# One head's query of the second attention moved from the attention block into the preparation block before it

## The reference

```python
h = _layernorm(x, axis=-1) * (1 + ca) + sa
q_c = rmsnorm(h @ w_qa, g_qa)                       # 192 wide
q = (q_c @ w_qb).reshape(b, s, NH, ND + RD).transpose(0, 2, 1, 3)
q_nope, q_rope = q[..., :ND], q[..., ND:]
kv = h @ w_kva
k_c, k_rope = rmsnorm(kv[..., :KVR], g_kva), kv[..., KVR:]
...
q_rope = q_rope * cos + rotate_half(q_rope) * sin
...
attn = softmax(query @ key.T * QK ** -0.5)          # 512 x 512 for each of 2 x 32 heads
x = x + ga * (attn @ v) @ w_o
```

## Time and profile before

| what | us |
|---|---|
| three runs: median | 921.61 |
| three runs: lowest, highest | 920.1, 924.47 |
| profiled execution, its own time | 919.29 |
| profiled execution, span from first to last instruction | 917.1 |
| TensorE busy in the span | 825.5 (90%) |
| VectorE, GpSimd, ScalarE busy | 681.8, 538.3, 536.6 |
| mean granted TensorE clock | 0.953 of full |

### The profile page before, as it was taken

The page is one execution under the profiler, slowest core; times in us unless marked ns, Lnnn a source line. Parts: engine busy times, 40 slices in busy tenths (PEclk is TensorE's granted clock), DMA queues, the critical chain, the costliest instruction groups (busy, mean ns, idle before and its releaser), DMA issues.

```text
span 917.1 us, 15064 instructions
## 1 busy us (share of the span) xinstructions
PE 825.5 (90%) x4560; PEld 543.2 (59%) x4560; DVE 681.8 (74%) x1322; ACT 536.6 (59%) x1158; POOL 538.3 (59%) x481
## 2 busy tenths in 40 slices
PE   3899994599996985799999999999899999999997
PEld 1678873577774763456565656565565656565443
DVE  4758987644453462989898989899998989898662
ACT  5658873724223772666666666666566666666522
POOL 3324342012122213999888888888788888887313
PEclk8789997799998895999999999999999999999999
DMA  8440000745233440466666666666567766666511
GB/s 331 168 156 1 2 2 2 217 130 173 88 103 126 136 129 18 119 157 155 153 154 154 156 154 155 150 155 153 129 153 184 184 148 155 152 154 146 130 37 69
DMA packets 91460, 120.08 MB, mean 131 GB/s; under 512 B 30386, under 2 KB 41650, under 8 KB 91380
## 3 DMA queue, kind: packets, MB, share of 16 engines
q1 hardware_dynamic: 66804, 85.54, 33.8%
q10 hardware_dynamic: 24576, 33.59, 14.8%
HBM read 41.45 MB, written 2.10 MB: 47 GB/s over the span
## 4 chain that ended last, share of the span: by engine, by line
PE 45%; DVE 9%; issue 5%; ACT 1%; ACTq 1%; POOL 1%; DMA 0%; POOLq 0%; DVEq 0%; SPq 0%
PE bank L1477 11%; PE bank L1464 6%; PE bank L1465 5%; PE bank L1466 5%; PE bank L1491 4%; PE bank L1493 3%; PE bank L1492 3%; PE bank L1535 3%; DVE blk L1595 2%; DVE cT_lo L1669 2%; DVE stage_a L1571 2%; ACTq L1406 1%; DVE nmax L1579 1%; PE bank L1450 1%; PE bank L1451 1%
## 5 line engine op out<-in xcount | busy, mean ns | idle before, releaser
L1579 DVE TENSOR_REDUCE nmax<-bank 128x1 f32<-128x512 f32 x256 | 173.9, 679 | 46.6 <-PE bank L1466 45.4
L1741 ACT ACTIVATE prob<-bank,nmax 128x512 f32<-128x512 f32 x172 | 118.3, 688 | 109.8 <-DVE nmax L1579 98.2
L1848 POOL TENSOR_TENSOR prob<-prob,rinv 128x512 f32<-128x512 f32 x129 | 132.5, 1042 | 37.5 <-DVE rinv L1587 36.0
L1464 PE MATMUL bank<-xk_hi,q_hi 128*128 128x512 f32 x256 | 113.0, 442 | 16.2 <-ACT prob L1741 8.4
L1595 DVE STREAM_TRANSPOSE blk<-prob 128x512 f32<-128x512 f32 x172 | 120.0, 698 | 6.7 <-ACT prob L1784 5.3
L1464 PEld LDWEIGHTS bank<-xk_hi,q_hi 128*128 128x128 f32 x256 | 48.5, 189 | 94.6 <-issue 52.2
L1465 PE MATMUL bank<-xk_lo,q_hi 128*128 128x512 f32 x256 | 101.6, 397 | 0.0
L1466 PE MATMUL bank<-xk_hi,q_lo 128*128 128x512 f32 x256 | 100.9, 394 | 0.0
L1843 POOL TENSOR_TENSOR q_lo<-stage_a,q_hi 128x512 fp32r<-128x512 f32 x64 | 82.0, 1282 | 26.4 <-ACT q_hi L1735 26.4
L1839 POOL TENSOR_TENSOR stage_a<-stage_a 128x512 f32<-128x512 f32 x64 | 82.9, 1295 | 7.0 <-DMA stage_a<-stage_a 6.2
L1741 ACT ACTIVATE stage_a<-bank,nmax 128x512 f32<-128x512 f32 x84 | 57.8, 688 | 49.1 <-DVE nmax L1579 42.8
(11 more groups left out here) (251 smaller groups left out, 1947.4 us busy)
## 6 DMA issues: line engine op xcount, KB each, us to landing
pT<-blk SPq DMA_DIRECT2D x256, 64.0 KB, 2.1
pT<-blk ACTq DMA_DIRECT2D x256, 64.0 KB, 2.1
raw_e<-blk SPq DMA_DIRECT2D x256, 64.0 KB, 2.1
raw_e<-blk ACTq DMA_DIRECT2D x256, 64.0 KB, 2.1
raw_e<-in_wo SPq DMA_DIRECT2D x16, 512.0 KB, 3.9
stage_a<-stage_a SPq DMA_DIRECT2D x128, 64.0 KB, 2.0
raw_e<-in_wmod SPq DMA_DIRECT2D x6, 1024.0 KB, 7.8
stage_a<-in_wmod SPq DMA_DIRECT2D x12, 512.0 KB, 4.4
```

The costliest lines, as they stand in the source:

```text
L1464: pe.matmul(sbk, q_hi[:, u % 2, q], xk_hi[:, 2, ks], start=True, stop=False)
L1579: dve.tensor_reduce(nmax[:, s % RING:s % RING + 1], s_bank[s % 2][:, :], AX.X, ALU.max, negate=True).then_inc(max_done, 1)
L1741: act.activation(prob[s % RING], s_bank[s % 2][:, :], ACT.Exp, bias=nmax[:, s % RING:s % RING + 1], accum_out=rsum[:, s % RING:s % RING + ...
L1848: pool.tensor_tensor(prob[s % RING], prob[s % RING], bc(rinv[:, s % RING:s % RING + 1], [P, S]), ALU.mult).then_inc(norm_pool, 1)
```

## The change

What one unit's q needs is defined ahead of both blocks, with semaphores and buffers; the functions are the ones of before (`weights` is now `act_weights` and `pool_weights`, `project` is `pe_project`), each taking its engine. Unit 0 then goes through them in the preparation block:

- SP loads `cosq` and `sinq` first and the couples behind them, and issues the swap of unit 0 at its end.
- ScalarE makes `w_hi` of couple 0 at the end of iteration 4 and `q_hi` of unit 0 at the end of iteration 6.
- GpSimd clears `qu` after tile 3's rest, makes `w_lo` of couple 0 after tile 5's, and has `q_sum(0)` and `q_rest(0)` after tile 7's.
- VectorE makes both parts of unit 0's rotation at the end of iteration 5.
- TensorE projects unit 0 at the end of iteration 5 and unit 1 at the end of iteration 7, into bank 7; the four gates go to iterations 0 to 3.

In the attention block `project(0)`, `project(1)` and all of unit 0's steps are gone. ScalarE and GpSimd begin with the weights of couple 1, VectorE with unit 1's rotation, SP with the swap of unit 1. The banks of PSUM and the parts of the staging buffer are dealt out anew: `qf` and `qu` lie where the raw latent weights were, and two of the six buffers of probabilities move.

```diff
+            qf, qu = stage_flat[:, 0:S], stage_flat[:, S:2 * S]
+            qs = sinq[0:KVR, :]
+            q_bank = bank[7]
+
+            def ge(eng, s_, v):
+                if v > 0:
+                    eng.wait_ge(s_, v)
+
+            def act_weights(act, j):
+                ge(act, q_ps, 2 * j)
+                p = j % HP
+                act.activation(w_hi[:, :, :, :], wq_all[:, 2 * p:2 * p + 2, :, :], ACT.Copy).then_inc(whi_done, 1)
+
+            def pool_weights(pool, j):
+                p = j % HP
+                pool.wait_ge(whi_done, j + 1)
+                pool.tensor_tensor(w_lo[:, :, :, :], wq_all[:, 2 * p:2 * p + 2, :, :],
+                                   w_hi[:, :, :, :].bitcast(F32), ALU.subtract).then_inc(wlo_done, 1)
+
+            def pe_project(pe, u):
+                b, p, e = u // NH, u // 2, u % 2
+                ts = slice(b * S, (b + 1) * S)
+                hi, lo = w_hi[:, e, :, :], w_lo[:, e, :, :]
+                if e == 0:
+                    pe.wait_ge(wlo_done, p + 1)
+                ge(pe, qrot, 2 * u)
+                pe.matmul(q_bank[:, :], hi[:, 0, :], xk_hi[:, 0, ts], start=True, stop=False)
+                pe.matmul(q_bank[:, :], hi[:, 0, :], xk_lo[:, 0, ts], start=False, stop=False)
+                pe.matmul(q_bank[:, :], lo[:, 0, :], xk_hi[:, 0, ts], start=False, stop=False)
+                pe.matmul(q_bank[:, :], hi[:, 1, :], xk_hi[:, 1, ts], start=False, stop=False)
+                pe.matmul(q_bank[:, :], lo[:, 1, :], xk_hi[:, 1, ts], start=False, stop=True).then_inc(q_ps, 1)
+
+            def swap(sp, u):
+
+                sp.wait_ge(qrot, 2 * u + 1)
+                ge(sp, qsum, u)
+                sp.dma_start(qu[KVR:KVR + 32, :], qs[32:64, :]).then_inc(swap_in, 16)
+                sp.dma_start(qu[KVR + 32:P, :], qs[0:32, :]).then_inc(swap_in, 16)
+
+            def rotate(dve, u, part):
+
+                if part == 0:
+                    dve.wait_ge(q_ps, u + 1)
+                    ge(dve, swap_in, 32 * u)
+                    dve.tensor_tensor(qs[:, :], q_bank[KVR:P, :], sinq[KVR:P, :], ALU.mult).then_inc(qrot, 1)
+                else:
+                    ge(dve, qlo_done, u)
+                    dve.tensor_tensor(qf[:, :], q_bank[:, :], cosq[:, :], ALU.mult).then_inc(qrot, 1)
+
+            def q_round(act, u):
+                act.wait_ge(qsum, u + 1)
+                ge(act, s_ps, (u - 1) * TPB)
+                act.activation(q_hi[:, u % 2, :], qf[:, :], ACT.Copy).then_inc(qhi_done, 1)
+
+            def q_sum(pool, u):
+                pool.wait_ge(qrot, 2 * u + 2)
+                pool.wait_ge(swap_in, 32 * (u + 1))
+                pool.tensor_tensor(qf[:, :], qf[:, :], qu[:, :], ALU.add).then_inc(qsum, 1)
+
+            def q_rest(pool, u):
+                pool.wait_ge(qhi_done, u + 1)
+                pool.tensor_tensor(q_lo[:, u % 2, :], qf[:, :], q_hi[:, u % 2, :].bitcast(F32),
+                                   ALU.subtract).then_inc(qlo_done, 1)
+
...
                 def gate_at(t):
-                    return t - 3 if 3 <= t <= 6 else None
+                    return t if t <= 3 else None
 
                 with nc.Block() as block:
                     @block.sync
                     def _(sp):
+                        sp.dma_start(cosq, a["cosq"]).then_inc(rot_in, 16)
+                        sp.dma_start(sinq, a["sinq"]).then_inc(rot_in, 16)
                         for j in range(FFN_COUPLES + 2, COUPLES // 2):
                             load_couple(sp, j)
-                        sp.dma_start(cosq, a["cosq"]).then_inc(rot_in, 16)
-                        sp.dma_start(sinq, a["sinq"]).then_inc(rot_in, 16)
-                        sp.wait_ge(rot_in, 64)
+                        sp.wait_ge(acc_set, 1)
+                        swap(sp, 0)
...
+                            if t == TPB:
+                                act_weights(act, 0)
+                            if t == TPB + 2:
+                                q_round(act, 0)
...
                             if (n := gate_at(t)) is not None:
...
+                            if t == TPB - 1:
+                                pool.wait_ge(split2_lo, wc_base + KC)
+                                pool.memset(qu[:, :], 0.0).then_inc(acc_set, 1)
+                            if t == TPB + 1:
+                                pool_weights(pool, 0)
+                        q_sum(pool, 0)
+                        q_rest(pool, 0)
...
+                            if t == TPB + 1:
+                                dve.wait_ge(rot_in, 64)
+                                for part in range(2):
+                                    rotate(dve, 0, part)
...
+                            if t in (TPB + 1, TPB + 3):
+                                if t == TPB + 1:
+                                    pe.wait_ge(gate1_done, 4)
+                                    pe.wait_ge(xklo_done, TPB)
+                                pe_project(pe, (t - TPB) // 2)
...
-            w_hi = sb("w_hi", [P, 2, 2, P], F32R, ph)
-            w_lo = sb("w_lo", [P, 2, 2, P], F32R, ph)
             b_hi = sb("b_hi", [P, D], F32R, ph)
             b_lo = sb("b_lo", [P, D], F32R, ph)
-            qf, qu = stage_flat[:, 2 * D:2 * D + S], stage_flat[:, 2 * D + S:2 * D + 2 * S]
-            qs = sinq[0:KVR, :]
...
-            prob = [prob_own[:, n, :] for n in range(RING - 2)] + [stage_flat[:, 0:S], stage_flat[:, S:2 * S]]
+            prob = [prob_own[:, n, :] for n in range(RING - 2)] + [stage_flat[:, 2 * S:3 * S], stage_flat[:, 3 * S:4 * S]]
...
-            s_bank, q_bank, ct_bank, o_bank = bank[0:2], bank[2], bank[3], bank[4:8]
+            s_bank, ct_bank, o_bank = bank[0:2], bank[2], bank[3:7]
...
-                    for u in range(4):
-                        swap(u)
+                    for u in range(1, 4):
+                        swap(sp, u)
...
                         move_ready(sp, u)
                         for n in range(SYNC_GROUPS * QD):
                             if n == 6 and u + 4 < UNITS:
-                                swap(u + 4)
+                                swap(sp, u + 4)
...
-                    project(0)
-                    project(1)
                     for s in range(STEPS):
                         if s < ROUNDS:
                             scores(s)
                         if s % TPB == 0 and s // TPB + 2 < UNITS:
-                            project(s // TPB + 2)
+                            pe_project(pe, s // TPB + 2)
...
-                    dve.wait_ge(acc_set, 1)
-                    for u in (0, 1):
-                        for part in range(2):
-                            rotate(u, part)
+                    for part in range(2):
+                        rotate(dve, 1, part)
...
                         if s % TPB in ROPE_AT and s // TPB + 2 < UNITS:
-                            rotate(s // TPB + 2, ROPE_AT[s % TPB])
+                            rotate(dve, s // TPB + 2, ROPE_AT[s % TPB])
...
-                    weights(0)
-                    q_round(0)
+                    act_weights(act, 1)
...
                         if st == 0 and u + 1 < UNITS:
-                            q_round(u + 1)
+                            q_round(act, u + 1)
...
-                        if s == 0:
-                            weights(1)
                         if s % 8 == 4 and s // 8 + 2 < COUPLES:
-                            weights(s // 8 + 2)
+                            act_weights(act, s // 8 + 2)
...
-                    pool.memset(qu[:, :], 0.0).then_inc(acc_set, 1)
-                    weights(0)
-                    q_sum(0)
-                    q_rest(0)
-                    q_sum(1)
+                    pool_weights(pool, 1)
+                    q_sum(pool, 1)
...
                         if st == 0 and u + 1 < UNITS:
-                            q_rest(u + 1)
-                        if s == 0:
-                            weights(1)
+                            q_rest(pool, u + 1)
                         if s % 8 == 4 and s // 8 + 2 < COUPLES:
-                            weights(s // 8 + 2)
+                            pool_weights(pool, s // 8 + 2)
...
                         if st == 3 and u + 2 < UNITS:
-                            q_sum(u + 2)
+                            q_sum(pool, u + 2)
```

More of the change, by code:

```diff
@@ L1118, in megakernel @@
             cosq, sinq = stage_flat[:, 2 * D + 2 * S:2 * D + 3 * S], stage_flat[:, 2 * D + 3 * S:2 * D + 4 * S]
+            w_hi = sb("w_hi", [P, 2, 2, P], F32R, ph)
+            w_lo = sb("w_lo", [P, 2, 2, P], F32R, ph)
+            whi_done = sem("whi_done")
+            wlo_done = sem("wlo_done")
+            q_ps = sem("q1_ps")
+            qrot = sem("qrot")
+            qsum = sem("qsum")
+            swap_in = sem("swap_in")
+            qhi_done = sem("qhi_done")
+            qlo_done = sem("qlo_done")
@@ new lines, in megakernel @@
+            acc_set = sem("acc_set")
+            s_ps = sem("s1_ps")
```

(56 more changed lines are left out.)

15 lines of the change are left out of this document (removed).

## The result

The changed kernel takes 905.9 us (median of 4 runs, 904.65 to 907.66) against 920.86 for the kernel before (4 runs, 916.12 to 924.47, three of them the ones known before the prediction). The medians lie 15.0 us apart; the ratio on record is 0.9864, 95% interval 0.9832 to 0.9897, that is 12.5 us less, within 9.5 to 15.5. A second timing gave 906.25 against 917.37, ratio 0.9877 (0.9848 to 0.9907), 11.3 us. Forecast were a gain of 12.9 and a time of 908.7, or 906.4 from the profiled execution. The profiled execution of the changed kernel took 904.65, with a span of 902.4.

The account below looks back on a forecast made before the run. The attention block's start was taken as bound by one chain of dependent steps. Gain 15.8 less costs 1.15 + 1.5 + 0.25 = 2.9 gives 12.9 us: from the median 921.61 to 908.7, range 904 to 915.

Parts of the forecast that it names:

- both holds: Attention block start: unit 0's q chain, and w_lo of couple 1 behind unit 1's q_lo; removing them gives 15.8 us.
- signs of being wrong: Attention block beginning before 345 or after 348, normalize later than 9 in, or the rest changing by over 2 us.
- What is removed: Attention block start: w_lo of couple 1 starts 0.7 us in, first normalize 7.6 instead of 23.4: 15.8 us less.
- GpSimd has 0.8 us to spare: Attention block: unit 1's q_lo ends at 6.8 us, ahead of the first normalize at 7.6.
- The table load: ScalarE in the attention block: 1.28 us, hidden under the first maxima; cost 0, without that cover up to 1.28.
- The preparation block: Added work makes the block end later by 1.15 + 1.5 + 0.25 = 2.9 us.
- the lock: Preparation block: tile 7's VectorE addition meets GpSimd's q_lo(0); 0.25 us, at worst a whole GpSimd operation, 1.26.
- the memset of `qu`: GpSimd in the preparation block, which works 7.6 of 37 us there: cost 0.
- Rival A: Attention block start: the granted clock falls late or never; gain 13.8 to 15.5, 906 to 908 us; chance 0.2.
- Rival B: Preparation block: late swap or tables slowing first loads, 3 to 4 us more; 911 to 913 us; chance 0.1.
- Rival C: Long later stretch gives the gain back: no change (917 to 924), chance 0.07, or slower (above 926), chance 0.04.
- Rival D: Attention block: w_lo(1) still runs behind q_lo(1), 6.1 us later; gain 6.8, 915 us; chance 0.03.

Follow-up runs that it names:

- q_hi(0) late: The changed kernel with unit 0's q_hi moved on ScalarE from the end of iteration 6 to the end of iteration 7, behind tile 7's squares; ratio 0.9842.
- again: The changed kernel timed and profiled once more, unedited; 906.25 us against 917.37, ratio 0.9877.
- added matmuls: The changed kernel with 16 matmuls whose results nobody reads, around tile 7's transposes and behind scores 0; ratio 0.9833 (two runs).
- 10 matmuls: The changed kernel with unit 0's q_hi behind tile 7's squares, unit 1's first rotation and swap in the preparation block, and ten unread matmuls; 901.95 us, ratio 0.9836.
- w(1) late: The changed kernel with w_hi and w_lo of couple 1 put back behind unit 1's q_hi and q_lo; ratio 0.9957.

## Why the prediction was right

The mechanism was the one forecast: both holds went, the early q cost the preparation block what was said, and in the edited stretch the gain is 12.4 and 12.0 us against 12.9. The nearness of the whole time is in part luck. The profiled executions differ by 14.7 us, since 4.0 us ahead of the change went one way and 1.7 behind it the other, and the interval of the ratio is 6 us wide. Two of the prediction's own signs of being wrong were met. The attention block began at 342.1 and 344.3, where before 345 was to count as wrong; the sign took the block's place for its length, though the place moves by 5 us with no edit ahead of it. And the rest from the first normalize took 1.7 and 2.4 us more than before, the second beyond the 2 us allowed. In the terms of the sum:

- *What is removed.* 15.8 forecast; 15.3 and 14.8 measured. The principle held: w_lo of couple 1 at 0.71. The step that was mis-sized is the cover given to unit 1's swap, "GpSimd has 0.8 us to spare": it counted a landing of 2.0 and it took 3.35 and 3.79. That is 1.35 and 1.79 more, less the 0.8 to spare 0.55 and 1.0, and the normalize came 0.5 and 0.95 behind the forecast 7.6. The 3.7 stood in the earlier trace rows and was used for unit 0's swap, not for this one.
- *The table load* ran from 342.75 to 344.03, and the first exponential at 344.24 waited for the maximum, 0.2 behind it: cost 0, as said, but with the slack nearly gone.
- *The preparation block*: 2.9 forecast, 2.9 measured, and its parts hold too. The rotation started 42.75 us behind the table load (335.15 - 292.33 = 42.8 forecast, with 2.8 for three gates that make 2.7), q_hi(0) at 47.7 (47.6), ScalarE waited 1.49 for it (1.5), the squares came at 48.2 (forecast 340.5 - 292.33 = 48.2). The last of tile 7's matmuls started at 46.37 (334.70), against 45.22 before (337.55): 1.15, the one projection. The addition took 0.38 instead of 0.17: 0.2 for the lock, 0.25 forecast. With q_hi(0) late the squares came 1.53 earlier, and the block gained 1.3: 1.5 and 0.2 less the 0.4 of the other lock. One term put at 0 was not nothing in its place: the memset of `qu` follows tile 3's rest on GpSimd, and VectorE's addition beside them took 0.82 (at 311.74) instead of 0.36. It didn't reach the block's end, whose parts above add up without it.
- *The lock.* The text gave a short term to it and a whole GpSimd operation as the worst case. Both were met: 0.2 in the changed kernel, and 1.29 for a two-element addition in the one with q_hi(0) late, of which 0.4 reached the block's end. The Trainium skill (SBUF — State Buffer, section Who interferes with whom) says that the other fully blocks, for a VectorE operation in its two-port mode; the traces agree in that each of these additions ends 0.02 to 0.03 us behind the GpSimd operation that it met (338.06 and 338.03, 340.41 and 340.38). Which mode they ran in no trace shows.
- *Rival A, the clock.* The granted clock was 1.00 through the block's first microsecond and 0.50 in 344 to 345; it fell some 1.8 us into the block (an estimate from the 0.96 in 343 to 344) against some 1.2 before (0.70 in 344 to 345): late, not never. The clock counted for nothing as long as the swap was the bound, and for 1.4 us once it was not. The Trainium skill's sentence (TensorE: Matmul & The Clock Gate, section What's actually happening) that activity releases the throttle agrees with these runs: with ten matmuls that nobody reads between the others the clock stayed at 1.00.
- *Rival B*: the longer landing came, in the attention block instead of the preparation block, at 0.5 to 0.95 us and not 3 to 4 (its gain of 8.6 to 11 doesn't follow from 3 to 4 us more, which would leave 8.9 to 9.9). *Rival C* did not come: the stretch behind is 1.7 and 2.4 us longer, where C wanted 8.8 and more. *Rival D* did not come either, and the run with the weights late shows what D would have been, 5.1 and 5.6 us more than the two profiles of the changed kernel, against the 6.1 that the text gave.

## What to carry to other kernels

When a chain at a block's start is moved away, look for the next thing that each engine's order puts behind it: here two holds of 7.0 and 5.6 us stood in one stretch, and moving either alone left the other. Read the slack that each remaining branch has and give every DMA on it its longest landing, not its median. And compare lengths between two marks of the edited stretch in several executions before a few us of a difference are believed.

## What the hardware did that was not expected

The second of the swap's two DMAs of 64 KB landed in 3.3 to 3.8 us in five profiles (changed 3.35, again 3.79, q_hi(0) late 3.32, added matmuls 3.69, 10 matmuls 3.3) and in 2.0 in the seven others (1.99 in both profiles of before, 2.03 in w(1) late). What tells the two groups apart is one packet of the instruction queue, of 0.02 MB, in the same microsecond as the swap's own. DMA queues of the changed kernel in 344 to 345 (packets, MB, share of 16 engines):

```profile
q1 hardware_dynamic: 77, 0.12, 50.0%
q8 instruction: 1, 0.02, 6.8%
```

In w(1) late that packet stood in 343.0 to 343.5, ahead of the swap's first in 345.5, and before in 344.0 to 344.5, five us ahead of it. With the swap in the preparation block it came some 2 us behind in two kernels (340.0 to 341.5 and 343.0 in the first of them); in the one with 10 matmuls it fell among the swap's again (342.5 to 343.0), and the swap took 3.3, beside the chain this time, so the normalize did not move. An estimate from the row: 6.8% of 16 engines for a microsecond is about 1.1 us of one engine. In the changed kernel the swap's last three packets came in 345.5 to 346.5, behind the rest. That the instruction packet holds back a few packets of the swap fits all twelve profiles; it was not tried by itself, so the cause is not shown.
